# Cross-attention with a key mask: four heads to a tile, two tiles added on GpSimd, one spread of the reciprocals for both

## What is computed

```
mask = attn_mask.astype(float32)                  # 16 x 1024 x 64, 0 or 1
qh = (q @ Wq + bq); kh = (k @ Wk + bk); vh = (v @ Wv + bv)     # 16 heads of 64
attn = einsum('bqhd,bkhd->hbqk', qh, kh) * mask
attn = exp(attn - max(attn)) * mask               # one maximum over everything
attn = attn / (sum(attn, axis=-1) + 1e-15)
out  = einsum('hbqk,bkhd->bqhd', attn, vh) @ Wo + bo
x    = out + residual                             # residual is q
return (x - mean) / sqrt(var + 1e-5) * gamma + beta
```

## Time and profile before

| | |
|---|---|
| median of 3 runs | 1641.56 us (1640.26 to 1642.91) |
| profiled execution, its own time | 1642.11 us |
| its span | 1640.3 us |
| scores phase, from the start to | about 874 us |
| output phase, its first sums in the loop to the end | 884 to 1640 us |
| PE busy | 1618.2 us (99%) |
| DVE, ACT, POOL busy | 1120.9 us (68%), 886.9 us (54%), 444.3 us (27%) |
| DMA queue of SP | 314.47 MB, 52.2% of 16 engines' span |

### The profile page before, as it was taken

One profiled execution on the slowest core, in us unless ns is written; L12 is line 12 of the kernel. 1 busy time (PEld: TensorE's weight loads), 2 busy tenths in 40 slices (PEclk: granted clock), 3 DMA queues, 4 the chain that ended last, 5 costly groups with the idle time before them and its releaser, 6 DMA issues. The chain is left out here.

```text
span 1640.3 us, 32372 instructions
## 1 busy us (share of the span) xinstructions
PE 1618.2 (99%) x11824; PEld 785.5 (48%) x11824; DVE 1120.9 (68%) x2253; ACT 886.9 (54%) x1357; POOL 444.3 (27%) x768
## 2 busy tenths in 40 slices
PE   7999999999999999999999999999999999999998
PEld 4555455555554555545544444444444444444443
DVE  6665564665646655556466988788878887888785
ACT  6555454554545545455446666655656565656542
POOL 0000000000000000000000565665566556655665
PEclk9999999999999999999999999999999999999999
DMA  7483534634554527354436765566556555665422
GB/s 241 158 299 120 195 150 155 244 123 162 185 175 176 178 104 256 130 186 160 136 154 254 300 229 196 221 256 244 199 222 256 193 203 218 256 243 199 173 78 78
DMA packets 81668, 315.95 MB, mean 193 GB/s; under 512 B 5408, under 2 KB 9760, under 8 KB 71840
## 3 DMA queue, kind: packets, MB, share of 16 engines
q1 hardware_dynamic: 81568, 314.47, 52.2%
HBM read 184.43 MB, written 130.02 MB: 192 GB/s over the span
## 5 line engine op out<-in xcount | busy, mean ns | idle before, releaser
L92 PE MATMUL ps_s<-x_hi,g_hi 128*128 128x512 f16 x1024 | 389.4, 380 | 2.7 <-issue 2.1
L101 PE MATMUL ps_o<-u,p_hi 128*128 128x512 f16 x1024 | 388.8, 380 | 1.3 <-DVE p_lo L1275 1.3
L93 PE MATMUL ps_s<-x_lo,g_hi 128*128 128x512 f16 x1024 | 388.6, 380 | 0.0
L94 PE MATMUL ps_s<-x_hi,g_lo 128*128 128x512 f16 x1024 | 388.6, 379 | 0.0
L102 PE MATMUL ps_o<-u,p_hi 128*128 128x512 f16 x1024 | 388.1, 379 | 0.0
L103 PE MATMUL ps_o<-u,p_lo 128*128 128x512 f16 x1024 | 388.1, 379 | 0.0
L595 ACT ACTIVATE s<-ps_s,c_bias 128x512 f32<-128x512 f32 x256 | 176.4, 689 | 353.9 <-PE ps_s L94 351.8
L737 DVE TENSOR_TENSOR score_max<-score_max,tile_max 128x1 f32<-128x1 f32 x257 | 40.7, 158 | 311.9 <-ACT s L595 309.4
L823 POOL PARTITION_ALL_REDUCE key_max<-early_max x1 | 0.7, 712 | 854.1 <-DVE early_max L746 854.1
L1403 POOL TENSOR_TENSOR y<-y,gamma_b 128x512 f32<-128x512 f32 x124 | 157.8, 1273 | 265.7 <-ACT y L1134 265.7
L1121 ACT ACTIVATE p_hi<-ps_bc 128x512 f16<-128x512 f32 x256 | 152.0, 596 | 139.9 <-DVE ps_bc L1269 139.8
(11 more groups left out here) (136 smaller groups left out, 2275.0 us busy)
## 6 DMA issues: line engine op xcount, KB each, us to landing
scores<-s SPq DMA_DIRECT2D x30, 2048.0 KB, 7.6
x<-xT_in SPq DMA_DIRECT2D x32, 1024.0 KB, 9.8
u_halves<-u_out SPq DMA_DIRECT2D x64, 512.0 KB, 4.3
u<-u_halves SPq DMA_DIRECT2D x16, 2048.0 KB, 10.6
s_more<-scores SPq DMA_DIRECT2D x16, 2048.0 KB, 9.7
y<-x_in SPq DMA_DIRECT2D x32, 1024.0 KB, 7.7
out<-y SPq DMA_DIRECT2D x31, 1024.0 KB, 5.1
s<-scores SPq DMA_DIRECT2D x14, 2048.0 KB, 9.4
```

The costliest lines, as they stand in the source:

```text
L92: pe.matmul(out, lhs_hi, rhs_hi, start=first, stop=False)
L93: pe.matmul(out, lhs_hi, rhs_lo, start=False, stop=False)
L94: return pe.matmul(out, lhs_lo, rhs_hi, start=False, stop=last)
L101: pe.matmul(out, lhs_hi, rhs_hi, start=False, stop=False, skip_group_check=True)
```

## The change

A tile now holds **four** heads and half of their keys: tile 2f holds keys 0 to 31 of heads 4f to 4f+3, tile 2f+1 keys 32 to 63 of the same heads. From this follow:

- POOL adds both tiles of a pair (`add_keys`, new, four a unit, 128x512 float32 each) into `e_both`, and from the third unit on PE sums the four results rather than the eight tiles (`sum_added`, new).
- Both tiles of a pair have the same reciprocals: a spread makes one product for two tiles, into the second half of the bank, and `scale_p` reads that half twice (`of_both_tiles`).
- The rows of a mask for the two halves of keys differ, and so `mask_add` now has both halves for one unit: `load_mask` brings 512 queries by four DMAs, for every unit rather than every batch, and `mask(g, u)` is done by DVE in every unit.
- The folded keys are written to other places (`of_folded`), the keys' biases are put in place by 8 small instructions instead of 2 (`bias_of`), and the folded values are stored by four DMAs where there was one (`store_u`), since rows of the tile go to two places.
- The wait for the folded keys in front of a tile of scores now covers both pairs of heads in it.

The diff's core:

```
-def sum_weights(pe, bank, sel_sum, scores, i):
...
+def sum_added(pe, bank, sel_sum, added, i):
+    for q in range(4):
+        th, f = q // 2, 2 * (q % 2) + i
         mm = pe.matmul(bank[32 * q:32 * q + 32, 0:TT // 2], sel_sum[:, i, :],
-                       scores[:, p, th * TT // 2:(th + 1) * TT // 2],
-                       start=(i == 0), stop=(i == 3), skip_group_check=True)
+                       added[:, f, th * TT // 2:(th + 1) * TT // 2],
+                       start=(i == 0), stop=(i == 1), skip_group_check=True)
...
+            f, h4 = four(p)[0], four(p)[1] + h
+            return g[:, f, :, :, :, keys_of(h4)].rearrange("r c b a k -> r (c b a) k")
...
-            def load_mask(b):
-                sp.wait_ge(mask_ready, b + 1)
-                for h in range(2):
-                    sp.dma_start(mask32[h * NK:(h + 1) * NK, :],
-                                 maskT[bass.ds(b, 1), :, :].rearrange("a k t -> (a k) t")).then_inc(mask_in, 16)
+            def load_mask(n, b, u):
+                t0 = (u % UB) * TT
+                sp.wait_ge(mask_ready, n + 1)
+                for h in range(4):
+                    sp.dma_start(mask32[keys_of(h), :, :],
+                                 maskT[bass.ds(b, 1), :, t0:t0 + TT].rearrange("a (s k) t -> (a k) s t", s=2))\
+                      .then_inc(mask_in, 16)
...
-                    sp.dma_start(u_d[bass.ds(g * GB + b, 1), :, 4 * q * D:4 * (q + 1) * D].rearrange("a p n -> p (a n)"),
-                                 u_out[:, q % 2, b, :, :, :].rearrange("r p k d -> r (p k d)"))\
-                      .then_inc(u_stored[q % 2], 16)
+                    for h in range(2):
+                        for half in range(2):
+                            f, h4 = four(q)[0], four(q)[1] + h
+                            rows = slice(h * NK + half * HALF, h * NK + (half + 1) * HALF)
+                            to = u_d[bass.ds(g * GB + b, 1), keys_of(h4), :]\
+                                .rearrange("a r (i t n) -> (a r) i t n", i=2, t=NP // 2)[:, :, 2 * f + half, :]
+                            sp.dma_start(to, u_out[rows, q % 2, b, :, :, :].rearrange("r p k d -> r p (k d)"))\
+                              .then_inc(u_stored[q % 2], 16)
...
                 for u in range(UNITS):
                     if not (last and u >= UNITS - 2):
                         load_x(g * UNITS + u + 2, g * GB + (u + 2) // UB, u)
-                    if u == 2 and not last:
-                        load_mask(g * GB + 2)
+                    if not (last and u == UNITS - 1):
+                        load_mask(g * UNITS + u + 1, g * GB + (u + 1) // UB, u + 1)
...
-            def mask(g, j):
-                b = g * GB + j
-                dve.wait_ge(mask_in, 32 * (b + 1))
+            def mask(g, u):
+                n = g * UNITS + u
+                dve.wait_ge(mask_in, 64 * (n + 1))
...
-                    if p == (NP // 2 + 1 if u < UNITS - 1 else 0) and u % UB == 1 and not (last and u == UNITS - 1):
-                        mask(g, (u + 1) // UB)
+                    if p == (NP // 2 + 1 if u < UNITS - 1 else 0) and not (last and u == UNITS - 1):
+                        mask(g, u + 1)
...
+            return ps_bc[j][:, HT:2 * HT].rearrange("r (a t) -> r a t", a=1).to_broadcast([P, 2, HT])
...
+                else:
+                    for i in range(2):
+                        pe.wait_ge(e_added, 4 * n + 2 * i - 6)
+                        mm = sum_added(pe, ps_sum, sel_sum, e_both[:, u % 2, :, :], i)
...
-                    for k in range(2):
-                        for j, pair, th in side_by_side:
...
+                    for j, tile, th in side_by_side:
+                        rows = slice(32 * (2 * th + tile // 4), 32 * (2 * th + tile // 4) + 32)
+                        mm = pe.matmul(ps_bc[j][:, HT:2 * HT], sel_bc[rows, tile // 2, th, :], r_all[rows, s, :],
+                                       start=True, stop=True, skip_group_check=True)
...
+            def add_keys(n, u, i):
+                f = (0, 2, 1, 3)[i]
+                pool.wait_ge(exp_done, 2 * n + i // 2 + 1)
+                e = scores_of(u)
+                pool.tensor_tensor(e_both[:, u % 2, f, :], e[:, 2 * f, :], e[:, 2 * f + 1, :], ALU.add).then_inc(e_added, 1)
...
                     for t in range(TB):
                         inv_std(g, u, t)
+                        if t < TB - 1 and not (last and u >= UNITS - 3):
+                            add_keys(n + 3, u + 3, t + 1)
+                        if t == TB - 1 and not (last and u >= UNITS - 4):
+                            add_keys(n + 4, u + 4, 0)
                         if not (last and u == UNITS - 1):
                             affine(g, u, t)
+            for i in range(TB):
+                add_keys(2, 2, i)
+            add_keys(3, 3, 0)
```

More of the change, by code:

```diff
@@ L125, in rows_of_values, with four, keys_of @@
     return rows_of(1 - h if p >= NP // 2 else h)
-def place(p):
-    return 2 * (p % (NP // 2)) + p // (NP // 2)
+def four(p):
+    return p // 2, 2 * (p % 2)
+def keys_of(h):
+    return slice(h * HALF, (h + 1) * HALF)
 def fold_head_outputs(pe, banks, v, w, tiles):
@@ L282, in load_sel @@
                 sp.wait_ge(w_lo_done, 16)
-                for i in range(2):
-                    sp.dma_start(w32[:, i, :], sel_bc_d[i]).then_inc(w_loaded(16 + i)[0], 16)
+                sp.dma_start(w32[:, 0, :], sel_bc_d).then_inc(w_loaded(16)[0], 16)
             def load_ctx(g):
@@ L611, in scores_out @@
                         split_weight(split_behind[u][p])
-                    if first and u == 3 and p in (3, 5):
-                        copy_sel(p // 4)
+                    if first and u == 3 and p == 3:
+                        copy_sel()
                     if p in quads(u, first):
@@ L716, in bias_of @@
             def bias_of(b):
-                for h in range(2):
-                    of_keys = dve.tensor_scalar(c_bias[rows_of(h), :, b], c_sum[rows_of(b), h, :], 1.0, None, ALU.mult)
-                of_keys.then_inc(c_ready, 1)
-            def mask(g, j):
-                b = g * GB + j
-                dve.wait_ge(mask_in, 32 * (b + 1))
[L726 to L730, removed]
+                for h4 in range(4):
+                    for half in range(2):
+                        rows = slice(b * NK + half * HALF, b * NK + (half + 1) * HALF)
+                        of_keys = dve.tensor_scalar(c_bias[keys_of(h4), half::2, b], c_sum[rows, h4 % 2, h4 // 2::2],
+                                                    1.0, None, ALU.mult)
+                of_keys.then_inc(c_ready, 1)
+            def mask(g, u):
+                n = g * UNITS + u
+                dve.wait_ge(mask_in, 64 * (n + 1))
+                of_both = mask_add[:, u % 2, :, :].rearrange("r a t -> r (a t)")
+                dve.tensor_scalar(of_both, mask32[:, :, :].rearrange("r a t -> r (a t)"), -MASKED, MASKED,
+                                  ALU.mult, ALU.add).then_inc(mask_ready, 1)
+                dve.wait_ge(mask_ready, n + 2)
+                dve.tensor_reduce(mask_min[:, :], of_both, axis=AX.X, op=ALU.min).then_inc(least_steps, 1)
+                dve.wait_ge(least_steps, 2 * n + 2)
                 dve.tensor_tensor(least[:, :], least[:, :], mask_min[:, :], ALU.min).then_inc(least_steps, 1)
@@ L1063, in unit @@
                     mm = add_product(pe, o_bank(first, u, t)[:, :], (p_hi[:, s, p, cols], p_lo[:, s, p, cols]),
-                                     (u2[:, b, place(p), 0, :], u2[:, b, place(p), 1, :]))
+                                     (u2[:, b, p, 0, :], u2[:, b, p, 1, :]))
                     if p == NP - 1:
@@ L1427, in columns @@
         return v.reshape(-1, P).T
-    sel_sum = np.zeros((P, NP // 2, 32), np.float32)
-    sel_bc = np.zeros((P, NP, 2, P), np.float32)
+    sel_sum = np.zeros((P, 2, 32), np.float32)
+    sel_bc = np.zeros((P, NP // 2, 2, P), np.float32)
     part = np.zeros((P, 2), np.float32)
     for k in range(COPIES):
-        for h in range(2):
-            for p in range(NP):
-                row, keys = 8 * k + 2 * (p % 4) + h, slice(h * NK, (h + 1) * NK)
-                sel_sum[keys, p % 4, row] = 1.0
+        for h in range(4):
+            for f in range(NP // 2):
+                row, keys = 8 * k + 4 * (f % 2) + h, slice(h * HALF, (h + 1) * HALF)
+                sel_sum[keys, f % 2, row] = 1.0
                 for th in range(2):
-                    q = 2 * th + p // 4
-                    sel_bc[32 * q + row, p, th, keys] = P_SCALE
+                    q = 2 * th + f // 2
+                    sel_bc[32 * q + row, f, th, keys] = P_SCALE
                     part[32 * q + row] = (-1.0 if k >= 1 else 0.0, -1.0 if k >= 2 else 0.0)
```

64 lines of the change are left out of this document (35 added, 29 removed).

## The result

The changed kernel takes **1695.9 us** (median of 4 runs, 1694.2 to 1700.5), the kernel before 1642.2 (median of 4 runs): a ratio of 1.0337, 95% interval 1.0324 to 1.0349. It is slower, as forecast, but by more than was forecast, and the time lies 21 us above the top of the range (1675).

The account below looks back on a forecast made before the run. PE, busy 99% of the span, was taken to bound the kernel. From 1642.1 us, less 33.3 saved, plus 3 for the start, 1 for small items and 39.2 for seven mask waits: 1652.0 us, range 1627 to 1675.

Parts of the forecast that it names:

- the chain: Fourth unit of a group: mask lands behind x, DVE splits keys late, PE's fold waits, then PE's clock is halved.
- the loss for each group: Scores phase, all groups but the last: PE's 4.3 us wait plus 1.3 us at reduced clock, 5.6 us, seven times.
- What PE saves: Output phase: fewer sum products save 25.8 us and fewer spread products 7.5 us, together 33.3 us (31 to 35).
- What hides the adds: Output phase: POOL's adds cost nothing in the loop, but delay PE's first sums once by 3 us (1 to 7).
- Small items of the first group: First group, where DVE also splits weights, plus 12 more bias instructions a group: 1 us (0 to 3).
- What the masks cost: Fourth unit of a group: mask lands at 440.4, behind x, so PE waits 4.3 us (2.7 to 6.3), seven times.
- The second price of a wait: After each PE wait its clock is granted at 0.50 for a stretch, costing 1.3 us (0 to 1.7).
- The hidden wait: Rival: the fourth unit's mask wait does not delay PE, so time is 1613 or a little less, 1609; chance 0.13.
- SP falls behind: Rival: more stores and mask loads make ACT wait for `u_out`, 3 us more a group, about 1675 to 1690; chance 0.06.
- the main case: Whole kernel: PE's saving outweighed by the mask waits, 1652.0 us, own range 1629 to 1674; chance 0.78.
- DVE and POOL block each other: Rival, output phase: each POOL add keeps DVE from its inputs, so DVE sets the pace, about 1703 us; chance 0.03.
- The weighing of short DMAs: Mask loads and stores: the short-transfer penalty was set aside because 2 KB rows ran at 356 GB/s, 4 KB at 315.

Follow-up runs that it names:

- e5: e2 with POOL's adds left out, so PE sums all eight tiles in every unit as before the change; 1638.7 us.
- e6: e2 with a spread again making a product for each tile into both bank halves, DVE reading the whole bank; 1621.05 us.
- e2: The changed kernel with DVE preparing the fourth unit's mask behind tile 5 rather than tile 0, SP's queue unchanged; 1614.2 us, ratio 0.9834.
- e3: The changed kernel with a batch's folded values stored by one DMA of 128 partitions, not four of 32; 1666.5 us, ratio 1.0155.
- e1: The changed kernel with SP loading the fourth unit's mask ahead of the third unit's scores rather than behind x; 1614.4 us, ratio 0.9837.
- e7: e2 with each add on POOL done twice, same result; 1691.65 us, ratio 1.0301.
- e8: The kernel before, with each store of folded values cut by columns into four DMAs of 128 rows of 1 KB; 1640.5 us, ratio 0.9995.
- e4: The kernel before, with each store of folded values cut by partitions into four DMAs of 32 rows of 4 KB; 1640.95 us, ratio 0.9996.

## Why the prediction was wrong, and what it had right

The sign and the chain were right; **one term was mis-sized, the loss for each group: 5.6 us forecast, at most 8, and 11.7 measured** (81.7 / 7). Of the 43.9 us between 1652.0 and 1695.9, 42.5 are this. By its steps:

- *What PE saves*, 33.3: 24.5 + 6.9 by `e5` and `e6`, and 31.4 for the phase. Right.
- *What hides the adds*: nothing in the loop waits for them, right. At the start I took 3 us; PE waited 1.1:

```profile
986.57 0.64 PE L96 MATMUL ps_both<-e_both,sel_sum 128*32 128x256 f32 x8 [1.08 <-POOL e_both L1459]
```

- *Small items of the first group*, 1 us: the first gap alone is 2.3. Everything but the seven waits comes to 1614.2 (`e2`), where the terms gave 1612.8.
- *What the masks cost*: this step failed, in the clause "for ten more DMAs in the way I add 0.4". I took the bytes at the rate of the earlier trace rows and forgot that each DMA is also issued: eight stores in 8.95 us, not two in 1.6. I had rows for an issue, 0.33 us for the scores and 1.05 for `x` in the earlier trace rows, and used them nowhere; the wider bound, "2 us for twelve short DMAs", is a sixth of a microsecond each. In the one group followed above DVE's wait of 12.1 us is made of 6.8 for order and bytes (forecast 6.1), 0.6 for the mask's short DMAs, and 4.7 for the stores. Of these, 1.5 are because SP still issues the second unit's 16 stores when the third unit's scores are ready: they are issued 1.67 us behind the last masked tile (463.22 to 464.89), and 0.17 in `e3` (452.71 to 452.88). Four stores take nearly as long there as the 16 (13.47 us against 13.92), because SP mostly waits for the folded values; but the four are done 4.0 us before the scores are issued, and the 16 only 0.3. The other 3.2 are the eight behind the scores. They hold back the issue of `x` by 6.8 us, and half of that is made good: `x` lands 8.0 us behind its issue, not 10.1 as in `e3`, and the mask is there 1.5 us behind `x`, not 3.0.
- *The second price of a wait*: 1.3 us taken, with 1.7 as the most; 1.7 to 2.0 measured, 1.2 of it in the folds. The bound came from the one stretch of 3.3 us in the earlier trace rows; the stretch at 0.50 shown above lasts 9.7 us, the most of it inside the wait.
- *The hidden wait*, the rival of 1609 to 1613: not what happened, but its price is what `e1` and `e2` measure, 1614.
- *SP falls behind*: right in part (the 1.5 us above). Its price, 1675 to 1690, is nearer to 1695.9 than the main case, but by chance: it stood for ACT waiting for `u_out` to be stored, and the profile has no such wait in the loop, only one of 2.8 us in the first group, where `e2` has one of 2.3 too. I counted 3 us of slack on SP; the 16 stores leave none.
- *DVE and POOL block each other*: refuted, by `e7` most of all. The Trainium skill's warning (Perfetto Trace Analysis, "Optimizing Scalar/DVE Operations") is not borne out by these runs. They test it only in part: each of DVE's 512-column operations in the loop of this phase reads at most one tile from SBUF and any other from PSUM, and no run has DVE read two large tiles from SBUF beside POOL's adds.
- *The weighing of short DMAs*: the rule of the Trainium skill (Perfetto Trace Analysis, "DMA Optimizations") was set aside by comparing rates with the DMA engines full. By it the wait would have been at the upper bound, 6.3, which is nearer than 4.3. The runs bear out that short DMAs pay for each transfer; but the price is paid on the queue that issues them, and rows of 1 KB (`e8`) and of 4 KB (`e4`) cost it the same.

What stays open: why the issue of a store with its rows in two pieces takes SP 0.58 us and not 0.32; what holds SP's issues close behind a store of 2048 KB; and how much slower, if at all, the data of a 32-partition store moves.

## What to carry to other kernels

When a layout change turns one DMA into four, count issues as well as bytes: find the row of the queue's own time for one, multiply, add what issues close behind a large transfer take, and see what is queued behind. Before a change is given up for a new wait, ask whether the waiting instruction can stand later on its in-order engine; here one condition was worth 82 us. A wait of PE cost 1.7 to 2.0 us more than its length here.

## What the runs showed of the hardware

- Stores of 128 KB in a row start 0.5 us apart on SP's queue, over 32 partitions (3.86 us for eight) or over 128 (3.49 for seven), and 0.77 apart with rows in two pieces (6.15 for eight). The issue alone takes about 0.33 us for 128, 512 or 2048 KB.
- Close behind a store of 2048 KB the same eight stores take 2.7 to 3.3 us more. Four loads of a mask take 2.09 us away from it and 4.13 close behind.
- Each of PE's seven waits, of 4 to 11 us, had a granted clock of 0.50 over the folds behind it (2.68 us for 48 products, 1.45 in `e2`), and cost 1.7 to 2.0 us on top of its length.
- A float32 add of 128x512 on POOL beside DVE left DVE's median at 688 ns (685 before) even with POOL busy for 96%, for operations that read at most one of their tiles from SBUF.
